# Routed experts of a recurrent / mixture / attention stack: other operand order for the fixed experts, other pass order, four buffers for down weights

## What is computed

```
x = x + tanh(g_xattn[0]) * wkv(time_decay, time_first, layernorm(x), ctx)
x = x + tanh(g_ffn[0])   * moe(layernorm(x))
x = x + tanh(g_xattn[1]) * attention(layernorm(x), ctx)
x = x + tanh(g_ffn[1])   * mx_ffn(layernorm(x))     # weights and rows quantised in blocks of 32

# moe: 64 experts, top 4 per row, expert width 64, and two shared experts
logits = flat @ router_w
topk_idx = top_k(logits + router_bias, 4)
g = silu(einsum('nd,edf->nef', flat, wg)); u = einsum('nd,edf->nef', flat, wu)
routed = einsum('ne,nef,efd->nd', comb, g * u, wd)
```

## Time and profile before

| | us |
|---|---|
| median of 3 runs | 512.68 (511.4 to 513.83) |
| the profiled execution | 514.03 |
| its span, first to last instruction | 512.3 |
| PE busy | 406.5 (79%) |
| PE weight loads busy | 289.6 (57%) |
| DVE busy | 351.4 (69%) |
| POOL busy | 247.5 (48%) |
| ACT busy | 181.4 (35%) |
| DVE, product of one pass (L1078), 32 times | 0.29 each |
| DVE, one piece of quantising (L1064 to L1072), 24 times | 3.05: the means 0.41, 0.44, 0.20, 0.48, 0.29, 0.39, 0.43, 0.43 |
| POOL, rescaling of one piece (L534), 24 times | 0.63 each |

### The profile page before, as it was taken

The page is one execution under the profiler, slowest core; times in us unless marked ns, Lnnn a source line. Parts: engine busy times, 40 slices in busy tenths (PEclk is TensorE's granted clock), DMA queues, the critical chain, the costliest instruction groups (busy, mean ns, idle before and its releaser), DMA issues.

```text
span 512.3 us, 8514 instructions
## 1 busy us (share of the span) xinstructions
PE 406.5 (79%) x2839; PEld 289.6 (57%) x2839; DVE 351.4 (69%) x840; ACT 181.4 (35%) x416; POOL 247.5 (48%) x347
## 2 busy tenths in 40 slices
PE   0476788778677899999699678768887899988884
PEld 0265666666446566677477456556665455555543
DVE  0568886656986455589577326857857699999992
ACT  0353465445301454444244242325354122222210
POOL 2356565423227577777441265866212245555451
PEclk9987798879959899999899699979997999999998
DMA  7999961112923597668954342433110000000000
GB/s 222 266 216 271 242 237 52 52 52 59 170 41 100 130 297 224 173 173 181 161 150 142 118 137 80 146 87 118 57 42 1 0 1 12 10 10 12 11 10 22
DMA packets 72314, 57.42 MB, mean 112 GB/s; under 512 B 38864, under 2 KB 64592, under 8 KB 72272
## 3 DMA queue, kind: packets, MB, share of 16 engines
q1 hardware_dynamic: 60880, 37.23, 27.9%
q0 software_dynamic: 4608, 12.59, 10.8%
q10 hardware_dynamic: 6784, 7.05, 4.1%
HBM read 42.18 MB, written 14.68 MB: 111 GB/s over the span
## 4 chain that ended last, share of the span: by engine, by line
PE 47%; issue 16%; DVE 15%; POOL 10%; ACT 3%; DMA 3%; ACTq 3%; another core or an unknown queue 2%; POOLq 0%; DVEq 0%
PE psum L1214 9%; PE psum L1380 6%; PE psum L1401 4%; PE psum L1237 3%; PE psum L1398 3%; POOL arena_dn L628 3%; PE psum L1371 3%; POOL mx_w L631 2%; PE psum L1224 2%; PE psum L1283 2%; DMA bias_bc<-_xattn_norm_k_img_w_dram 2%; PE psum L1229 2%; PE psum L1281 2%; PE psum L1470 2%
## 5 line engine op out<-in xcount | busy, mean ns | idle before, releaser
L542 POOL DMA_INDIRECT shared<-h_dram,tok_u x64 | 66.9, 1046 | 49.9 <-PE psum L1214 22.3
L1501 PE MATMUL psum<-arena_dn 128*128 128x512 f32 x128 | 57.1, 598 | 3.2 <-ACT arena_dn L785 3.2
L628 POOL TENSOR_TENSOR arena_dn<-arena_dn 128x512 f32<-128x512 f32 x16 | 20.3, 1271 | 45.6 <-DVE arena_dn L1047 45.6
L1501 PEld LDWEIGHTS psum<-arena_dn 128*128 128x128 f32 x128 | 23.7, 190 | 31.2 <-issue 26.3
L566 POOL DMA_INDIRECT arena_up<-ys_dram,slot_u x32 | 31.4, 981 | 14.1 <-issue 14.1
L1078 DVE TENSOR_TENSOR h1T<-psum,h1T 128x128 f32<-128x128 f32 x32 | 9.3, 292 | 40.0 <-ACT h1T L733 37.4
L1214 PE MATMUL psum<-ident,mx_w 128*128 128x128 f32 x128 | 23.3, 312 | 16.2 <-POOL mx_w L631 8.9
L1214 PE MATMUL psum<-ident,arena_dn 128*128 128x128 f32 x96 | 18.3, 310 | 21.8 <-DVE arena_dn L878 19.3
L1214 PE MATMUL psum<-ident,arena_up 128*128 128x128 f32 x144 | 25.0, 292 | 12.4 <-DVE arena_up L1105 2.9
L1214 PEld LDWEIGHTS psum<-ident,mx_w 128*128 128x128 f32 x128 | 16.8, 158 | 27.1 <-POOL mx_w L631 10.9
L1596 PE MATMUL psum<-arena_dn,mx_w 128*128 128x256 f32 x128 | 30.1, 390 | 0.4 <-ACT mx_w L795 0.3
(11 more groups left out here) (226 smaller groups left out, 1065.4 us busy)
## 6 DMA issues: line engine op xcount, KB each, us to landing
ys_dram<-stage SPq DMA_DIRECT2D x32, 256.0 KB
arena_up<-in_L_ffn_wg_dram SPq DMA_DIRECT2D x8, 512.0 KB, 8.3
arena_up<-in_L_ffn_wu_dram SPq DMA_DIRECT2D x8, 512.0 KB, 7.4
h1T<-in_L_ffn_wd_dram SPq DMA_DIRECT2D x64, 64.0 KB
arena_dn<-in_L_ffn_wd_dram SPq DMA_DIRECT2D x3, 1024.0 KB, 11.5
va_dram<-stage ACTq DMA_DIRECT2D x8, 256.0 KB, 3.7
kT_dram<-stage ACTq DMA_DIRECT2D x8, 256.0 KB, 4.6
arena_up<-kT_dram SPq DMA_DIRECT2D x8, 256.0 KB, 2.7
```

Source lines behind the costliest of these rows:

```text
L542: pool.indirect_dma_start(out=xg[n % 4][:, b, :], out_offset=None, in_=h1_dram[:, :], in_offset=bass.IndirectOffsetOnAxis(ap=tok_u[:, 2 * ...
L628: pool.tensor_tensor(haF[h], haF[h], heF[h], ALU.subtract).then_inc(sem("hint"), 1)
L1501: ins = pe.matmul(bank[2 * part + h][:, :], xTF[n % 2][:, c, :], mx_gu[:, c, lo:lo + HW], start=(c == 0), stop=(c == C - 1))
```

## The change

For fixed passes the operands swap: an expert's 128 columns are stationary, its 64 gathered rows move, and the result has the hidden index on partitions (up in the lower half, gate in the upper, hence the swapped order of `wu` and `wg`). SiLU and product are made on 64 x 256, and the down products take `hb` straight as their stationary side: turns and copies of hidden values remain in chosen passes only. For chosen passes each of four experts is applied to all 128 rows of its group, into an area of its own (a full bank of 512 columns per pass), and DVE picks the rows by two products on 64 partitions each. So `xgT` needs no zeros. The down products move one step earlier: step k ends with those of k - 1, fixed or chosen; in chosen steps the hidden turns of k - 1 stand right behind the up products of k. ACT's order follows: copies of hidden values first, then SiLU of k, rows of k + 1, read-out of k - 1. The loop is one step shorter. `dnS` gets four buffers (over the down weights of the first experts, which by then are used up) and SP requests three passes ahead; `xg` gets five buffers; the scales of the quantising get four instead of two; the halves are spread evenly, three in two passes.

```diff
 def weight_halves(n):
-    return min(max(min(n, NPS - 1), 0) + 2 * max(n - NPS + 1, 0), 2 * NWC)
+    return min(max(3 * n // 2, 0), 2 * NWC)
...
+        XG = 5
+        xg = [take(2, D) for _ in range(XG)]
+        take = carver(arena_dn)
+        DN = 4
+        dnS = [take(2, D) for _ in range(DN)]
...
             def dn_load(n):
-                s = n % 2
-                if n >= NPS + 2:
-                    sp.wait_ge(sem("mo_y"), n - 1)
+                s = n % DN
+                sp.wait_ge(sem("mo_y"), max(n - DN + 1, DN))
...
             for n in range(NP):
-                if NPS <= n + 2 < NP:
-                    dn_load(n + 2)
+                if NPS <= n + DN - 1 < NP:
+                    dn_load(n + DN - 1)
@@ POOL @@
+                    if n == 4:
+                        pool.wait_ge(sem("sdown"), T)
-                    reach(pool, sem("xgT_ps"), n - 3)
+                    reach(pool, sem("xgT_ps"), n - XG + 1)
...
-                due = min(weight_halves(n - 5) // 2, NWC)
+                due = weight_halves(n - 7) // 2
@@ ACT @@
-            for k in range(-1, NP + 2):
+            for k in range(-1, NP + 1):
+                n = k - 1
+                if NPS <= n:
+                    act.wait_ge(sem("hT_ps"), n - NPS + 1)
+                    reach(act, sem("mo_y"), n - 1)
+                    turned = bank[k % 2][0:F, 0:4 * S].rearrange("p (b n) -> p b n", b=2)
+                    act.copy(hbT[n % 2][0:F, :, 0:S], turned[:, :, 0:S])
+                    act.copy(hbT[n % 2][F:2 * F, :, S:P], turned[:, :, S:P]).then_inc(sem("hbT"), 1)
                 if 0 <= k < NP:
                     act.wait_ge(sem("gu"), k + 1)
                     reach(act, sem("hb"), k - 1)
+                    if k < NPS:
+                        act.activation(sgb[k % 2][0:F], bank[2 + k % 2][F:2 * F, 0:4 * S], ACT.Silu).then_inc(sem("sgb"), 1)
+                    else:
+                        act.activation(sgb[k % 2].rearrange("p (x f) -> p x f", x=4),
+                                       bank[2 + k % 2].rearrange("p (x n f) -> p x n f", x=4, n=2)[:, :, 1, :],
+                                       ACT.Silu).then_inc(sem("sgb"), 1)
...
-                n = k - 2
+                n = k - 1
                 if n >= 0:
+                    reach(act, sem(f"ys_out{n % 2}"), 16 * (n // 2))
                     act.wait_ge(sem("mo_y"), n + 1)
@@ DVE @@
+                    if n < NPS:
+                        dve.tensor_tensor(hb[n % 2][0:F], bank[2 + n % 2][0:F, 0:4 * S], sgb[n % 2][0:F], ALU.mult)
+                    else:
+                        dve.tensor_tensor(h3[0:S, :, 0:F], up3[0:S, :, 0:F], sg3[0:S, :, 0:F], ALU.mult)
+                        dve.tensor_tensor(h3[S:P, :, 0:F], up3[S:P, :, 2 * F:3 * F], sg3[S:P, :, F:2 * F], ALU.mult)
@@ PE @@
             def up_fixed(k):
+                for x in range(2 * Q):
+                    b, at = x // Q, slice(x % Q * S, x % Q * S + S)
+                    for c in range(C):
+                        ins = pe.matmul(bank[2 + k % 2][:, x * S:(x + 1) * S], moe_up[:, c, 2 * Q * k + x, :],
+                                        xgT[k % 2][:, b, c, at], start=(c == 0), stop=(c == C - 1))
+            def up_chosen(k):
+                for x in range(2 * Q):
+                    for c in range(C):
+                        ins = pe.matmul(bank[2 + k % 2][:, 2 * F * x:2 * F * (x + 1)], xgT[k % 2][:, x // Q, c, :],
+                                        moe_up[:, c, bass.ds(chosen[x], 1), :].rearrange("p a f -> p (a f)"), ...)
+            def hidden_turn(n):
+                pe.wait_ge(sem("hb"), n + 1)
+                reach(pe, sem("hbT"), n - NPS)
+                for b in range(2):
+                    ins = turn(bank[1 - n % 2][0:F, b * P:(b + 1) * P], hb[n % 2][:, 2 * b * F:(2 * b + 1) * F])
...
-            for k in range(-1, NP + 2):
+            for k in range(-1, NP + 1):
                  # up products of k
+                if k > NPS:
+                    hidden_turn(k - 1)
                 # turns of the gathered rows of k + 1
-                n = k - 2
-                if n >= 0:
-                    down(n)
-                n = k - 1
-                if 0 <= n < NP:
-                    # turns of the hidden values of n
+                if 1 <= k <= NPS:
+                    down_fixed(k - 1)
+                elif k > NPS:
+                    down_chosen(k - 1)
```

More of the change, by code:

```diff
@@ L132, in build_program @@
         stage = sb("stage", [P, 2048])
-        xgT1 = stage[:, 0:1024]
-        ysb = [stage[:, 1024 + 512 * i:1536 + 512 * i].rearrange("p (b d) -> p b d", b=2) for i in range(2)]
         shared = sb("shared", [P, 3072])
@@ L217, in build_program @@
         kTS = [stage[:, 512 * b:512 * b + 512].rearrange("p (g n) -> p g n", g=4) for b in range(2)]
-        vaS = [t.rearrange("p b d -> p (b d)").rearrange("p (h d) -> p h d", h=H) for t in ysb]
+        vaS = [stage[:, 1024 + 512 * b:1536 + 512 * b].rearrange("p (h d) -> p h d", h=H) for b in range(2)]
         take = carver(arena_up[:, 6144:8192])
@@ L263, in build_program @@
         take = carver(shared)
-        xg = [take(2, D) for _ in range(4)]
-        xgT = [xgT1.rearrange("p (b c j n) -> p b c j n", b=2, c=C, j=Q), take(2, C, Q, P)]
+        XG = 5
+        xg = [take(2, D) for _ in range(XG)]
+        take = carver(stage)
+        xgT = [take(2, C, P) for _ in range(2)]
+        ysb = [take(2, D) for _ in range(2)]
         take = carver(h1T[:, :, :].rearrange("p c n -> p (c n)"))
-        sgb = [take(2, F) for _ in range(2)]
-        hb = [take(2, F) for _ in range(2)]
+        sgb = [take(4 * S) for _ in range(2)]
+        hb = [take(4 * S) for _ in range(2)]
         hbT = [take(2, P) for _ in range(2)]
-        dnS = [take(2, D) for _ in range(2)]
-        def own(tile):
-            return tile.rearrange("p x j (k n) -> p x (j k) n", n=S)[:, :, 0:Q * Q:Q + 1, :]
+        take = carver(arena_dn)
+        DN = 4
+        dnS = [take(2, D) for _ in range(DN)]
         take = carver(arena_up)
@@ L321, in build_program @@
         wam = sb("wam", [P, WC // QB])
-        wac = [sb(f"wac{i}", [P, WC // QB]) for i in range(2)]
+        wac = [sb(f"wac{i}", [P, WC // QB]) for i in range(4)]
         war = sb("war", [P, WC // QB])
@@ L358, in _, with up_load @@
                              swd[s].rearrange("(f p) n -> p f n", p=P)).then_inc(sem("shared_in"), 16)
-            def up_load(c, experts, into, parts=((0, wg), (1, wu))):
+            def up_load(c, experts, into, parts=((0, wu), (1, wg))):
                 for n, w in parts:
@@ L409, in _ @@
                 if n in (2, 3):
-                    up_load(0, (48,), "moe_in3", parts=((n - 2, (wg, wu)[n - 2]),))
+                    up_load(0, (48,), "moe_in3", parts=((n - 2, (wu, wg)[n - 2]),))
                 if n in (5, 6, 7, 8):
@@ L1086, in _ @@
             dve.wait_ge(sem("gu"), NG // 2)
[L1087 removed]
+            dve.wait_ge(sem("pad"), 8)
             dve.wait_ge(sem("gob"), 4)
@@ L1373, in up_fixed @@
                 ins.then_inc(sem("gu"), 1)
             def up_chosen(k):
-                experts = experts_of(mybir.EngineType.PE, k)
-                for b in range(2):
-                    for j in range(Q):
-                        for c in range(C):
-                            ins = pe.matmul(bank[2 + k % 2][:, 2 * F * b:2 * F * (b + 1)], xgT[k % 2][:, b, c, j, :],
-                                            moe_up[:, c, bass.ds(experts[Q * b + j], 1), :].rearrange("p a f -> p (a f)"),
-                                            start=(j == 0 and c == 0), stop=(j == Q - 1 and c == C - 1))
@@ L1383, in up_chosen @@
-                ins.then_inc(sem("gu"), 1)
-            def down(n):
-                pe.wait_ge(sem("hbT"), n + 1)
+                chosen = experts_of(mybir.EngineType.PE, k)
+                for x in range(2 * Q):
+                    for c in range(C):
+                        ins = pe.matmul(bank[2 + k % 2][:, 2 * F * x:2 * F * (x + 1)], xgT[k % 2][:, x // Q, c, :],
+                                        moe_up[:, c, bass.ds(chosen[x], 1), :].rearrange("p a f -> p (a f)"),
+                                        start=(c == 0), stop=(c == C - 1))
@@ L1390, in down, with down_chosen @@
                     pe.wait_ge(sem("moe_in2"), 16 * 2)
-                if n >= NPS:
-                    pe.wait_ge(sem(f"dn_in{n % 2}"), 64 * ((n - NPS) // 2 + 1))
+                reach(pe, sem("ysb"), n - 1)
+                for x in range(2 * Q):
+                    b, at = x // Q, slice(x % Q * S, x % Q * S + S)
+                    ins = pe.matmul(bank[4 + 2 * (n % 2)][at, b * D:(b + 1) * D], hb[n % 2][0:F, x * S:(x + 1) * S],
+                                    moe_dn[:, 2 * Q * n + x, :], start=True, stop=True)
+                ins.then_inc(sem("mo_y"), 1)
+            def down_chosen(n):
+                pe.wait_ge(sem("hbT"), n - NPS + 1)
+                pe.wait_ge(sem(f"dn_in{n % DN}"), 64 * ((n - NPS) // DN + 1))
```

(14 more changed lines are left out.)

76 lines of the change are left out of this document (29 added, 47 removed).

## The result

The changed kernel took 559.6 us (median of 4 executions, 552.5 to 562.5) against 512.8 us beside it: 1.082 times as long, 95% interval 1.074 to 1.091. This ratio compares the two shorter of the four executions (552.5 and 557.0), as the two longer ones, the profiled one among them, lie over 1.5% above the shortest; by the medians it is 1.091. I had forecast 507.2. The profiled execution took 562.2 (span 560.5). Later, on other chips, the same file took 1.0075 times as long as the kernel before (1.003 to 1.012) and 1.009 times (1.002 to 1.016). So there are two results to explain, a large one that comes and goes and a small one that stays.

A forecast was written before the change was run, and what follows sets the result against it. PE's own sequence was taken to set the clean cycle, with stalls for down weights and the ys store; 3.6 - 4.3 + 2.0 - 4.8 - 2.0 = -5.5 us gave 508.5, adjusted to the median 507.2, range 502 to 515.

The forecast's parts named there:

- term +3.6: Fixed stage: up products take 1.86 us, cycle 3.40 against 3.12, so +3.6 us, bounds 0 to +7.
- a bound and a rival: Fixed stage: 0.2 us more per cycle than its parts; upper bound +7; rival that it loses nothing, 503.6 us, chance 0.10.
- bound of +7: Fixed stage: upper bound, 0.2 us more in each cycle, as the old cycle of 3.18 had over its parts.
- -4.3: Chosen passes: 15 clean cycles of 3.99 us, 59.9 against 64.17, so -4.3 us before residual stalls.
- +2.0: Chosen passes: residual stalls left after four buffers absorb most of 9.6 us, +2.0 us, bounds 0 and 9.6.
- the rival of the lost cover: Chosen passes: late ys stores delay hidden copies and down products, residue 15.1, net +7.6, 520.3 us, chance 0.14.
- the stalls stay: Chosen passes: late transfers or SP's pace keep the stalls, residue 9.6, net +2.1, 514.8 us, chance 0.20.
- term -4.8: End of the expert stage: last up products to next stage take 6.78 us instead of 11.60, so -4.8 us.
- -2.0: Next stage's first three groups of turns: at higher clock after less PE idling, -2.0 us, bounds 0 and -2.7.

The follow-up runs named there:

- e1: Changed kernel with 12 filler products of 256 columns before the down products of steps 6 and 11 of the expert stage: 543.2 us in one execution.
- e2: Changed kernel with the fixed up products streaming all 128 gathered rows, half of the result unread: 513.3 us, ratio 1.010.
- m2: Stand-alone PE kernel, clock down at each start, products and pass copies: with 64 moving columns 0.50 throughout 154 us; with 128, begun at 406.66, 1.0 from 410.7.
- s1: Changed kernel with ScalarE's SiLU of pass 0 repeated 15 times as a stall made on purpose: 553.0, 555.0, 509.1 and 511.3 us.
- s2: Kernel before the change with a stall made on purpose, 19 repeats of its shorter SiLU: 503.0 us, ratio 1.015.
- b1: Kernel before the change, unaltered, on a chip without the natural stall: 493.9 us in one execution.
- a2: Changed kernel, unaltered, on a chip without the natural stall: 499.7 us, ratio 1.009.
- e5: Changed kernel with filler products in steps 0 to 2 and the chosen expert numbers read ahead of PE's wait: 511.6 us, ratio 1.038.
- e3: Kernel before the change with only four buffers for chosen down weights, requested three passes ahead: 506.7 us, ratio 0.997.
- m1: Stand-alone PE kernel without waits, each stretch begun with the clock up: 180 instructions took 20.04 us with 64 moving columns, 20.10 with 128.

## Why the prediction was wrong, step by step

**The fixed stage, term +3.6, was +49.4 where it counted.** The 1.86 us for the up products was right at full clock (1.83, 1.84), and so was the cycle (3.38 for 3.40). The step that failed is the one that priced this term: I took the cycle from rows at clock 1.0 and never asked whether the new instructions would run there. At the clock that they got, 0.50, the cycle was 6.36. I had seen the idle stretch ("the first three passes are held up by ACT, not by PE; I leave them") and left it because its cost was in both kernels. Its cost was not: the kernel before comes back from it in three passes, the new one not until the chosen passes. e1, e2, m2 and s1 with s2 show this from four sides; why ACT stalled, and why two of s1's executions got away, stays open. The Trainium skill, "TensorE: Matmul & The Clock Gate", Part 1, says that sustained matmul activity releases the throttle; by it 154 us of unbroken products should have, and the run of m2 disagrees for 64 moving columns behind a 128-column float32 load.

**The same term without the stall was +6.5, not +3.6.** b1 beside a2, first to 17th up products: 48.17 against 54.68. My 3.12 for the old cycle (37.40 us over twelve) was true of that profile only; b1 has 2.96 nearly throughout. I had noticed that the 3.18 was 0.2 over the sum of its parts, and used it as a bound and a rival in place of distrusting it. The 0.2 lies between the hidden turns and the next up products (0.54 us in the first profile, 0.34 in b1); why is open. So +6.5 is inside the bound of +7, but for another reason: the old cycle was shorter, the new one wasn't longer.

**Chosen passes, terms -4.3 and +2.0, were +1.0 (a2 against b1: 63.10 and 62.42, +0.7).** The cycle was 4.24, not 3.99. Up products to the hidden turns 1.89 (1.95), turns to down products 0.99 (1.03), down to up 1.36 instead of 1.01. What I missed is that PE reads the expert numbers between its wait for `xgT` and its first product; e5 moved that read and got 1.01 and 3.89. The residue was zero, not 2.0, but for a first cycle of 5.78 that was partly at the low clock, and the rival of the lost cover has not come: in the chosen passes of the first profile ACT never waited for a store.

**The stalls of the fifteen cycles were not a loss that buffers could remove.** Fifteen chosen cycles took 62.4 us in b1, 61.1, 62.1 and 63.6 with more buffers, 61.7 and 63.6 with cycles of 3.90, and 63.1 with cycles of 4.24. PE's pace differs by 9 us and the stage by 2.5. Windows of b1:

```profile
221.00:229.00 8.00, 8.00 (x68) 6.37 (x68) 7.28 (x20) 3.79 (x11) 5.79 (x7) 1.00 0.80 197
237.00:245.00 8.00, 6.27 (x53) 5.01 (x53) 5.52 (x16) 3.33 (x9) 5.07 (x6) 1.00 0.90 150
```

The DMA engines are busier there and move fewer GB/s; the quicker versions lose their lead near 240 to 260 us. That the transfers set the stage's length is argued from this and from the stage's times; no run changes the transfers. My rival "the stalls stay" had the likely reason for the wrong kernel: the change doesn't stall, and I take that to be because its cycle is long enough. So in these cycles neither the gain of four buffers nor the slower cycle shows in the sum. What four buffers do save lies behind them: with them alone (e3) the end took 8.12 us and the next three groups 2.67. What makes the transfers slow there I haven't tested.

**The end, term -4.8, was -4.65** (6.95 for 6.78; in a2 7.00 against b1's 10.00, -3.0). **The clock of the next stage, -2.0, was -0.8**, and the old value was mis-sized: 5.29 us takes its end from the chain and its start from the timeline, where start to start is 5.13. After the last chosen passes its first two groups still ran at half clock (1.52 and 1.70 us). In a2 all three were at full clock, 2.67 against b1's 5.17, -2.5. The end was right in mechanism and size; of the clock I had said that the first turns would be at 1.0, which came in a2 and not in the first profile. Why not there is open: PE's idle stretches ahead of them are the same 0.62 to 0.75 us in both.

So on a chip without the stall: +6.5 +0.7 -3.0 -2.5, +0.2 ahead of the stage and +2.1 behind it, 4.0 us of span, where I had -5.5. The bounds of my own terms added up to -11.8 and +7.5, so 501 to 520; the range that I gave, 502 to 515, was narrower. Two slips changed nothing: VectorE's work a pass comes to 2.5 us from the numbers beside it, not 2.7, and the upper bound of 2.1 for the up products uses the 0.13 of the four weight loads, while the four matmuls in 0.66 us that it names give 0.165 and 2.6.

## What to carry to other kernels

A product's duration read at full clock holds only where the new instructions can also bring the clock back: look for the last idle stretch ahead of the passes that change, and ask what the first passes behind it stream. Before pricing stalls as removable, see whether the whole stage keeps its length in a kernel whose own pace is slower. Take the old cycle from more than one execution when its parts don't add up to it.

## What the runs showed of the hardware that I had not expected

- PE, 100% busy with 128-column float32 loads and 64 moving columns, held a clock of 1.0 for the 20 us that the stretch ran (m1), and left one of 0.50 where it was for 154 us (m2). With 128 moving columns the same stretch was back at 1.0 after 4.0 us.
- One program can have two durations some 44 us apart on one chip (s1: 509, 511, 553, 555), with the same instructions.
- In the profiles of before, after, e1, e2 and e3 one of ACT's first two SiLUs came late (ACT idle 5.2 to 8.3 us, no engine named), and each time POOL stood still too (1.8 to 2.4 us, no engine named) and went on 0.3 us behind ACT; in none of the later ones, on three other chips. The kernel before took 510 to 513 us there and 497 to 499 elsewhere. No row names the cause.
